# Inverse square roots on GpSimd, an affine step on ScalarE, and another order of work inside the slot

## The reference, cut to what matters

```python
xn = layernorm(x)                                  # x: 8 x 256 tokens x 128
s  = recurrence(xn)                                # s_t = s_{t-1} A^T + uB_t, y = s C^T + D
h  = xn
for i in range(6):                                 # 6 layers
    h = attn(shift(h), Wqkv[i], qs[i], ks[i], Wo[i]) + h
    h = ffn(shift(h), g[i], b[i], W1[i], b1[i], W2[i], b2[i]) + h
out = x + s * silu(h)

# attn: q = q / max(norm(q), 1e-12) * qs, the same for k (16 heads of 64), rotary tables,
#       window attention (blocks of 32 queries on 64 keys, softmax), then @ Wo
# ffn:  xn = (x - mu) / sqrt(var + 1e-5) * g + b
#       (a * gelu(gate)) @ W2 + b2, with a, gate = split(xn @ W1 + b1)
```

## Time and profile before

| | |
|---|---|
| median of three runs | 1910.44 us (1904.49 to 1916.37) |
| the profiled execution: its own time | 1909.64 us |
| its span, from first to last instruction | 1907.8 us |
| mean granted TensorE clock | 0.984 of full speed |
| busy: PE / DVE / ACT / POOL | 1716.4 us (90%) / 1468.1 (77%) / 1095.4 (57%) / 1088.4 (57%) |
| chain that ended last | PE 57%, ACT 15%, issue 15%, DVE 11% |
| instruction fetch queue (q8) | 255 packets, 4.18 MB |

### The profile page before, as it was taken

How to read it: one execution, slowest core, us unless ns; L and a number is a source line. 1 busy time by engine, 2 the same in 40 slices (tenths; PEclk the granted TensorE clock), 3 DMA queues, 4 the chain that set the end, 5 groups by cost and what they waited for, 6 DMA issues and landing times.

```text
span 1907.8 us, 75895 instructions
## 1 busy us (share of the span) xinstructions
PE 1716.4 (90%) x30558; PEld 1209.9 (63%) x30558; DVE 1468.1 (77%) x2727; ACT 1095.4 (57%) x2035; POOL 1088.4 (57%) x970
## 2 busy tenths in 40 slices
PE   5689999999989999999999998999998999999986
PEld 2356666666666666666666666666666666666664
DVE  4688787878877877877887887777887888787764
ACT  2255665656655565656656665656665566566653
POOL 0366665556656655655666666565655655665540
PEclk9699999999999999999999999999999999999999
DMA  2122223222222322222322222222222232222222
GB/s 97 29 78 63 55 57 77 64 66 71 58 48 72 77 69 49 69 57 57 78 63 67 65 62 55 77 64 69 66 55 55 67 77 65 71 58 56 53 54 67
DMA packets 82897, 122.09 MB, mean 64 GB/s; under 512 B 25168, under 2 KB 28752, under 8 KB 82256
## 3 DMA queue, kind: packets, MB, share of 16 engines
q1 hardware_dynamic: 82512, 116.84, 24.4%
HBM read 20.28 MB, written 2.10 MB: 12 GB/s over the span
## 4 chain that ended last, share of the span: by engine, by line
PE 57%; ACT 15%; issue 15%; DVE 11%; ACTq 1%; DMA 0%; DVEq 0%; SPq 0%
PE QKb L450 12%; PE F L573 10%; PE O L510 9%; PE S L498 6%; PE VTb L473 5%; PE S L450 4%; ACT L665 3%; ACT E L665 3%; PE F L596 3%; ACT v_tok L676 3%; PE F L597 2%; PE S L521 2%; PE S L491 2%; ACT KT L659 2%; DVE hid L904 2%
## 5 line engine op out<-in xcount | busy, mean ns | idle before, releaser
L975 POOL TENSOR_TENSOR t<-t 128x512 f32<-128x512 f32 x384 | 488.2, 1271 | 426.1 <-DVE t L835 425.8
L835 DVE TENSOR_TENSOR t<-QKb,table 128x1024 f32<-128x1024 f32 x384 | 469.2, 1222 | 285.0 <-ACT sq L650 281.1
L969 POOL TENSOR_TENSOR t<-t,rn 128x512 f32<-128x512 f32 x384 | 413.7, 1077 | 178.0 <-DVE rn L896 170.9
L450 PE MATMUL QKb<-wq_sb,x_sh 128*128 128x512 f32 x768 | 413.3, 620 | 60.9 <-DVE t L835 51.8
L650 ACT ACTIVATE sq<-QKb 128x512 f32<-128x512 f32 x384 | 229.1, 597 | 332.9 <-PE QKb L450 332.8
L473 PEld LDWEIGHTS VTb<-cst,t 128*128 128x128 f32 x1536 | 193.7, 142 | 204.1 <-issue 202.3
L960 POOL TENSOR_TENSOR E<-E,rs 128x512 f32<-128x512 f32 x192 | 200.2, 1043 | 159.9 <-DVE rs L868 159.9
L510 PE MATMUL O<-PT,V 64*64 64x32 f32 x12288 | 232.2, 221 | 39.6 <-issue 38.1
L682 ACT COPY OT<-O 128x512 f32<-128x512 f32 x192 | 112.5, 586 | 263.8 <-PE O L510 263.8
L510 PEld LDWEIGHTS O<-PT,V 64*64 64x64 f32 x12288 | 205.9, 135 | 62.4 <-issue 43.7
L473 PE MATMUL VTb<-cst,t 128*128 128x128 f32 x1536 | 232.6, 274 | 0.3 <-issue 0.3
(11 more groups left out here) (136 smaller groups left out, 2197.5 us busy)
## 6 DMA issues: line engine op xcount, KB each, us to landing
V<-v_tok SPq DMA_DIRECT2D x1440, 64.0 KB, 2.0
wq_sb<-in_wqkv SPq DMA_DIRECT2D x36, 256.0 KB, 3.1
wo_sb<-in_wo SPq DMA_DIRECT2D x6, 512.0 KB, 3.6
w_sb<-in_w SPq DMA_DIRECT2D x6, 341.0 KB
w_sb<-in_w SPq DMA_DIRECT2D x6, 192.0 KB
y_spill<-OT SPq DMA_DIRECT2D x1, 1024.0 KB, 4.8
V<-y_spill SPq DMA_DIRECT2D x1, 1024.0 KB, 8.0
out<-V SPq DMA_DIRECT2D x4, 256.0 KB, 2.9
```

The lines of the kernel that those rows point to most:

```text
L450: return pe.matmul(out_, x_sh[:, pr, P * tile:P * (tile + 1)], wq_sb[:, col:col + 512], start=True, stop=True)
L835: dve.tensor_tensor(t12[:, v, :, :].rearrange("p c (h d) -> p c h d", h=8), QK_ps.rearrange("p (h d) -> p h d", h=8).unsqueeze(1) .to_broa ...
L969: pool.tensor_tensor(w, w, rn[:, vv // 4, 8 * (vv % 4):8 * (vv % 4 + 1)].unsqueeze(2) .to_broadcast([P, 8, DH]), ALU.mult).then_inc(qk_nor ...
L975: pool.tensor_tensor(w, w, t12[:, v, 1, :].rearrange("p (h c d) -> p h c d", h=8, c=2)[:, :, ::-1, :], ALU.add).then_inc(add_done, 1)
```

## The change

Sums of squares and inverse norms keep 32 columns per half. POOL puts the floor under them and raises them to the power -0.5 against a tile of -0.5, in two instructions behind its multiplication in slots 1 and 5 (`L_RN` = 5), and multiplies by the result in the next slot. The variances get a tile of their own; POOL raises them to -0.5 and makes the diagonal in slot 4 (`F_DIAG` = 28). `newton` is gone. The layer norm's times g plus b goes from DVE to ACT, behind the copy of the attention output in slot 7 (`F_AFF` = 31). ACT's `xq` goes behind the copy of the transpose, its `xs` copies ahead of the copy of the attention output. DVE's `cent` goes ahead of `hidden` for chunk 2. On PE (moves that the cut diff below does not repeat, like those of `xq` and `xs`) the first scan piece of a slot goes behind the projection, and Wo ahead of the second scan piece, mean, W2, variance and broadcast. DMAs stay as they are.

```diff
-L_SS, L_NEWTON, L_SCALE, L_TR = 2, 5, 6, 7
+L_SS, L_RN, L_SCALE, L_TR = 2, 5, 6, 7
...
+F_WO, F_MID, F_MEAN, F_CENT, F_SQ, F_VAR, F_VCOPY, F_DIAG = 19, 23, 25, 26, 26, 26, 27, 28
+F_BC, F_XN, F_AFF, F_W1, F_GEL, F_HID, F_W2, F_END = 30, 31, 31, 32, 32, 33, 34, 35
...
@@ PE, step @@
-                    recurrence(in_fill(s, v, 0))
                     if live(g, UNITS):
...
                         project(QK_ps, par, tile, QK_COLS[2 * half + kind]).then_inc(qk_ready, 1)
+                    recurrence(in_fill(s, v, 0))
...
@@ ACT, step @@
+                    f, pr = batch(s, par, v, F_AFF)
+                    if f is not None:
+                        if pr == 0:
+                            wait(act, in_ffn, (f // B + 1) * 48)
+                        wait(act, xr_done, f + 1)
+                        act.activation(xc[:, :], xc[:, :], ACT.Identity, bias=prm[:, R_B:R_B + 1],
+                                       scale=prm[:, R_G:R_G + 1]).then_inc(xn_done, 1)
...
@@ DVE, step @@
                     if f is not None:
                         hidden(f, pr, [0, 1])
+                    f, pr = batch(s, par, v, F_CENT)
+                    if f is not None:
+                        wait(dve, mean_ready, f + 1)
+                        wait(dve, w1_ready, f * NCH)
+                        dve.tensor_tensor(xc[:, :], xs[:, :], BANK_MEAN[:, 0:N], ALU.subtract)\
+                           .then_inc(cent_done, 1)
                     f, pr = batch(s, par, v, F_W2)
                     if f is not None:
                         hidden(f, pr, [2])
...
-                        wait(dve, nw_seq, ln_newton_count(f))
-                        dve.tensor_tensor(diag[:, :, :], ident.unsqueeze(1).to_broadcast([P, NT, P]), rstd,
-                                          ALU.mult).then_inc(diag_done, 1)
...
-                        dve.tensor_scalar(xc[:, :], xc[:, :], prm[:, R_G:R_G + 1], prm[:, R_B:R_B + 1],
-                                          ALU.mult, ALU.add).then_inc(xn_done, 1)
...
                         wait(dve, var_ready, f + 1)
-                        dve.tensor_scalar(ss[:, LN_HALF, NORMS:], BANK_VAR[:, 0:NT], 1e-5, None, ALU.add)\
+                        wait(dve, rstd_done, f)
+                        dve.tensor_scalar(var[:, :], BANK_VAR[:, 0:NT], 1e-5, None, ALU.add)\
...
                         wait(dve, sq_done, u + 2)
+                        if vv % 4 == 0:
+                            wait(dve, rn_done, rn_count(st - 1, vv // 4))
                         dve.tensor_reduce(ss[:, vv // 4, 8 * (vv % 4):8 * (vv % 4) + 16],
...
-                    if vv % 4 == 0 and (live(u, UNITS) or f is not None):
-                        newton(st, vv // 4, u, f)
...
@@ POOL, step @@
+                    u, vv, st, pr = unit(s, par, v, L_RN)
+                    if live(u, UNITS) and vv % 4 == 0:
+                        wait(pool, ss_done, upto(st * (SLOTS // 2) + 2 * (vv // 4) + 2, UNITS // 2))
                     u, vv, st, pr = unit(s, par, v, L_SCALE)
                     if live(u, UNITS):
                         if vv % 4 == 0:
-                            wait(pool, nw_seq, newton_count(st, vv // 4))
+                            wait(pool, rn_done, rn_count(st, vv // 4))
...
+                    if live(u, UNITS) and vv % 4 == 0:
+                        half = vv // 4
+                        pool.tensor_scalar(ss[:, half, :], ss[:, half, :], 1e-24, None, ALU.max).then_inc(ss_floored, 1)
+                        wait(pool, ss_floored, rn_count(st, half))
+                        wait(pool, qk_norm, upto((st - 1) * SLOTS + 4 * half + 4, UNITS))
+                        pool.tensor_tensor(rn[:, half, :], ss[:, half, :], minus_half[:, :], ALU.pow).then_inc(rn_done, 1)
+                    f, pr = batch(s, par, v, F_DIAG)
+                    if f is not None:
+                        wait(pool, var_copied, f + 1)
+                        pool.tensor_tensor(rstd[:, :], var[:, :], minus_half[:, 0:NT], ALU.pow).then_inc(rstd_done, 1)
+                        wait(pool, rstd_done, f + 1)
+                        pool.tensor_tensor(diag[:, :, :], ident.unsqueeze(1).to_broadcast([P, NT, P]),
+                                           rstd[:, :].unsqueeze(2).to_broadcast([P, NT, P]),
+                                           ALU.mult).then_inc(diag_done, 1)
                     if live(g, UNITS):
                         wait(pool, t12_done, g + 1)
```

More of the change, by code:

```diff
@@ L10 @@
 BF16 = mybir.dt.bfloat16
-I32 = mybir.dt.int32
 ALU = mybir.AluOpType
@@ L171, in gated_mix_kernel @@
         t12 = sb("t12", [P, 8, 2, 512])
-        ss = sb("ss", [P, 2, NORMS + NT])
-        rn = sb("rn", [P, 2, NORMS + NT])
-        nwt = sb("nwt", [P, NORMS + NT])
+        ss = sb("ss", [P, 2, NORMS])
+        rn = sb("rn", [P, 2, NORMS])
+        minus_half = sb("minus_half", [P, NORMS])
+        var = sb("var", [P, NT])
+        rstd = sb("rstd", [P, NT])
         QT = sb("QT", [P, 2, HP, N])
@@ L234, in gated_mix_kernel @@
         qk_ready, sq_done, t12_done, ss_done = sem("qk_ready"), sem("sq_done"), sem("t12_done"), sem("ss_done")
-        add_done, nw_seq, qk_norm = sem("add_done"), sem("nw_seq"), sem("qk_norm")
+        add_done, ss_floored, rn_done, qk_norm = sem("add_done"), sem("ss_floored"), sem("rn_done"), sem("qk_norm")
         tr_ready, tr_evac, v_ready, v_evac = sem("tr_ready"), sem("tr_evac"), sem("v_ready"), sem("v_evac")
@@ L274, in moved, with rn_count @@
             return st * len(v_moves(c // 2)) * 16
[L276 to L287, removed]
+        def rn_count(st, half):
+            return 2 * st + half + 1
         SCAN = scan_pieces()
@@ L531, in step @@
                         project(V_ps, pr, c // 2, V_COLS[c % 2]).then_inc(v_ready, 1)
+                    for k in range(QPS):
+                        f, pr = batch(s, par, v, F_WO + k)
+                        if f is not None:
+                            if k == 0:
+                                if pr == 0:
+                                    wait(pe, in_wo, (f // B + 1) * 16)
+                                wait(pe, var_copied, f)
+                            wait(pe, o_evac, f * QPS + k + 1)
+                            for h in (2 * k, 2 * k + 1):
+                                mm = pe.matmul(BANK_WO[:, 0:N], wo_sb[:, h, :], OT[:, pr, h, :],
+                                               start=(h == 0), stop=(h == HP - 1))
+                            if k == QPS - 1:
+                                mm.then_inc(wo_ready, 1)
                     recurrence(in_fill(s, v, 1))
@@ L562, in step @@
                                   start=True, stop=True).then_inc(bc_ready, 1)
[L564 to L576, removed]
                     f, pr = batch(s, par, v, F_W1)
@@ L642, in step @@
                     g = s * SLOTS + v
[L643 to L646, removed]
                     if live(g, UNITS):
@@ L660, in step @@
                                  VT_ps.rearrange("p (i q) -> p i q", i=4)).then_inc(tr_evac, 1)
+                    f, pr = batch(s, par, v, F_SQ)
+                    if f is not None:
+                        wait(act, cent_done, f + 1)
+                        act.activation(xq[:, :], xc[:, :], ACT.Square).then_inc(xq_done, 1)
                     a, k, st, pr = quad(s, par, v, L_EXP)
@@ L676, in step @@
                         act.copy(v_tok[:, c // 2, 512 * (c % 2):512 * (c % 2 + 1)], V_ps).then_inc(v_evac, 1)
+                    f, pr = batch(s, par, v, F_MID)
+                    if f is not None:
+                        wait(act, mid_done, f + 1)
+                        act.copy(xs[0:64, :], xm[0:64, pr, :]).then_inc(xs_done, 1)
+                        act.copy(xs[64:P, 1:N], xm[64:P, pr, 0:N - 1]).then_inc(xs_done, 1)
                     a, k, st, pr = quad(s, par, v, L_PV)
@@ L682, in step @@
                         act.copy(OT[:, pr, 2 * k:2 * k + 2, :], O2[:, :, 0:N]).then_inc(o_evac, 1)
[L683 to L687, removed]
                     if v == 5 and live(s + 1, STEPS):
@@ L808, in step @@
                            .then_inc(mid_done, 1)
-                    f, pr = batch(s, par, v, F_CENT)
-                    if f is not None:
-                        wait(dve, mean_ready, f + 1)
-                        dve.tensor_tensor(xc[:, :], xs[:, :], BANK_MEAN[:, 0:N], ALU.subtract)\
-                           .then_inc(cent_done, 1)
                     f, pr = batch(s, par, v, F_XN)
@@ L938, in _ @@
             pool.wait_ge(set_pool, 4)
+            pool.wait_ge(set_dve, 4)
+            pool.wait_ge(in_cst, 16)
             def zero_first_keys(pr):
```

45 lines of the change are left out of this document (8 added, 37 removed).

## The result

The changed kernel takes **1992.7 us** (median of 4 runs, 1986.8 to 1997.2) against 1907.8 (1904.5 to 1916.4) for the kernel before on the same chip: 1.044 times as long, 95% interval 1.039 to 1.049. The forecast was 1877, a gain; the change is a loss of 85 us. The profiled execution took 1988.9, with a span of 1987.1.

A forecast was written before the change was run, and what follows sets the result against it. It took PE's own list, plus waits for one excursion per step through DVE and ACT, as the bound. From 1909.6, minus 78, plus 54, minus 8 gave 1878, stated as 1877 us for the median; range 1860 to 1893.

The forecast's parts named there:

- POOL's power (hidden): POOL, slots 1 and 5: floor and power take 1.7 us, within slack of 3.9 and 3.3, so cost nothing.
- the sign of being wrong: POOL's power: the forecast is wrong if the power's mean is above 3 us.
- rival B: POOL's list in slots 5 and 1 ends after PE wants its transpose; at 5 us, 2003 us; chance 0.12.
- Slot 7 (loss): PE's W1 waits for the affine step behind ACT's copy: 1.19 us per step, 54 us lost.
- Slots 2 and 3 (gain): PE's waits for `hid`, `t`, `v_tok` go: 2.0 us in a step without gaps, 1.73 on average, 78 us gained.
- the case that it summed: Power hidden on POOL, W1 in slot 7 waiting for the affine step on ACT: 1877 us.
- Scan: Slots 1 to 10 of the beginning: projection goes ahead of the scan piece, 8 us gained, 0 to 12.
- Rival C: ACT reloads tables for Identity in slots 7 and 0, 1.28 us each: 1935 us; chance 0.04.
- A: No change: gain in slots 2 and 3 only equals slot 7's new wait; 1902 us, or 1910 without scan; chance 0.20.
- D: Better: PE's wait in slot 7 lets fetch catch up, gaps shrink by half: 1858 us; chance 0.08.

The follow-up runs named there:

- the old order: Kernel before, its order and W1 in slot 7 kept, with only powers, the variances' tile and diagonal moved to POOL: 2108.5 us.
- the one with products: Changed kernel with each of its 96 POOL powers turned into a product of the same operands, inverse roots left out: 1765.7 us.
- the new order alone: Kernel before with only the new statement order on PE, ACT and DVE: 1795.9 us with W1 in slot 0, 1843.6 with W1 in slot 7.

## Why the prediction was wrong, by its steps

**"POOL's power (hidden)": this step failed, by 227 us.** It took 1.7 us, DVE's time for the same function, for floor and power, between bounds of 0.07 each and 8.3. They take 0.29 + 0.08 + 5.46 = 5.83, and the power's mean of 5.46 is the sign of being wrong that the prediction named (above 3 us). The slack that it named for slot 5, 3.3, was right: 5.83 - 3.3 = 2.5, and PE waits 2.46. For slot 1 it named 3.9 and would have had 1.9 of waiting; measured is 0.65, so the slack is 5.2 there: with W1 in slot 0 that slot is 4.42 us long instead of 3.14, and the transpose comes those 1.3 us later. With W1 in slot 7, in the old order, the wait is 1.80. The error was one of reasoning, not of reading: DVE's time was taken for POOL because it did the same work, although no row said that the two engines are alike in it, while the bounds reached far past the threshold. The Trainium skill (GPSIMD Engine Reference, Engine selection) gives about twice DVE's time for an add, multiply or max of two inputs, and the prediction drew an estimate of 3.3 from it. The row names no power. Measured, floor and power took 5.83 / 1.66 = 3.5 times as long as the eight instructions of the earlier trace rows that do the same, so the rule does not carry over to this instruction. A range with both signs in it should have followed, with rival B at far more than 0.12.

**Rival B was the mechanism**, with its place and its threshold, and its 5 us was nearly the length. That its 2003 lies 10 us from the measured 1992.7 is luck: at 5.83 its own count gives 2.5 + 1.9 = 4.4 us per step, some 200 us in all and about 2075, and it is the place of W1, which it did not see, that brings this down. It also did not have the second part of the price. The spans of the changed kernel and of the one with products differ by 223.5 us, and three terms make 225.5: PE's waits for POOL's `t`, 134.6; PE's own instructions, 1752.0 - 1673.2 = 78.8, with the granted clock at 0.952 instead of 0.984; and gaps ahead of the product with V, 33.2 - 21.1 = 12.1. Most of the second term is the clock: in the trace's record of it PE was busy at the 0.50 level for 166.6 us, against 43.5 with products, and half of that difference is 62 us. The remaining 17 were not traced further; part is that groups behind a wait run longer (0.66 us for four transposes instead of 0.60). The waits cost PE more than themselves.

**"Slot 7 (loss)": a misreading of the diff.** It let W1 wait in slot 7 and took 54 us. The lag says slot 0. For the case that it described the sizes were fair: slots 7 and 0 took 1.36 us more per step on the mean of steps 6 to 46 (9.19 to 10.55), where it had 1.19; the affine step, 0.60 instead of 0.42, was at the upper bound that it had given. But the changed kernel has nearly no such wait (3.0 us in 3 places), and W1 in slot 0 takes 104 us off (1869.5 to 1765.7), nearly twice the loss that I had charged.

**"Slots 2 and 3 (gain)": right.** In the case that it summed slots 2 and 3 fell from 5.43 + 5.37 to 4.25 + 4.64 on the mean, 1.91 per step where it had 1.73; in a step without gaps 10.93 became 8.76, 2.17 where it had 2.0. What it did not see is that the gain has two keys: the new order alone gives 1.26 of it (4.91 + 4.63), with Newton still on DVE.

**Scan: right.** The projection that opens the fifth step came at 171.7 us in that case, 181.2 before: 9.5 us, the whole beginning included, where it had 8.

**Rival C is out**: ACT has its two table loads per step, 47 each, and the affine step runs between them as `L687` in 0.60 us. Rivals A and D were about the case with W1 in slot 7. There 1869.5 lies outside A, and of D's halved gaps ahead of the product with V little came: 31.7 us, from 38.1.

Two errors of opposite sign stand in the forecast. For the case that it summed, without the power's cost and with W1 in slot 7, it had 1877, and that ran in 1869.5. From there the move of W1 takes off 104 us and the power adds 227, which leads to 1992.7. These two are differences of the same runs, so that they close proves nothing more. Without the power's error the forecast would still have missed by 111 us, on the other side; that the misread slot of W1 made its miss smaller, 116 us instead of some 220, is chance. (Its terms as written add to 1878.4 for the median; 1877 is a slip of one.)

## What to carry to other kernels

Before work moves to another engine, its time there is taken from that engine's rows; where it has none for the operation, the forecast hangs on the threshold of its slack, and has to be given for both sides of it. Read every changed lag constant in a diff as a moved instruction, and ask which slot it now fills and whom it feeds earlier: here the one constant was worth 48 to 128 us, and the move of Newton 0 to 25. And waits on TensorE can be paid twice: here 135 us of them came with 79 us more in its own instructions, some 62 of them from the clock.

## What the runs showed of the hardware

- A power of two tensors on GpSimd took 0.71 us for 2 columns, 2.93 for 16 and 5.46 for 32, all on 128 partitions: a line through the first and the last is 0.39 plus 0.158 per column, and it gives 2.92 for 16. A product of the full width of 512 took 1.04.
- VectorE's instruction on 128x32 took 1.04 and 0.97 us beside a GpSimd tensor instruction, and 0.18 and 0.19 alone, each time ending 0.04 to 0.05 after GpSimd's did. Over the whole run the mean of `L874` was 857 ns with Newton in slots 0 and 4, and 191 ns in slots 1 and 5:

```profile
L874 DVE TENSOR_SCALAR rn<-ss 128x32 int32<-128x32 int32 x96 | 82.3, 857 | 6.8 <-DVE ss L871 2.0
```

  The Trainium skill (SBUF — State Buffer, Who interferes with whom) says that a VectorE instruction with two SBUF inputs, or in a two-port mode, waits for the whole of a GpSimd instruction that came first; these rows agree.
- An affine step by Identity with a scale and a bias per partition took 0.60 us for 128x256 on ScalarE, a square of the same size 0.42.
- After PE had been idle for 2.46 us and busy again for about 1.7 us, the granted clock was 0.50 for near 7 us (1087.3 to 1094.1), and a projection took 2.07 us instead of 1.02. After another wait of 2.46 us, until 1163.24, it stayed at 1.00. Over the run with the powers the clock stood at 0.50 for 192 us in all, with products for 59.
